# First attention of a two-layer kernel: probabilities scaled one period later, a shorter first guess, the bias as a matrix product

## The reference, cut to what matters

```python
q = _ln((x @ Wq + bq).reshape(b, s1, H, HD), qn_w, qn_b)
k = _ln(kv[..., :HD], kn_w, kn_b)        # the first 48 keys of a batch
k_dca = _ln(kv_dca[:, :, 0], kn_dca_w, kn_dca_b)   # its last 16 keys
...
ctx = _attn(qT, k, v)                    # softmax over 48 keys
ctx_dca = _attn(qT, k_dca, v_dca)        # softmax over 16 keys
return (ctx + ctx_dca) @ Wo + bo
```

## Time and profile before

| | |
|---|---|
| median of 3 runs | 749.72 us (747.78 to 749.95) |
| the profiled execution | 747.85 us, its span 746.0 us |
| busy in the span | PE 668.1, DVE 556.2, ACT 480.1, POOL 442.4 us |
| mean granted clock of TensorE | 0.979 of 2.4 GHz |

### The profile page before, as it was taken

How to read it: one execution, slowest core, us unless ns; L and a number is a source line. 1 busy time by engine, 2 the same in 40 slices (tenths; PEclk the granted TensorE clock), 3 DMA queues, 4 the chain that set the end, 5 groups by cost and what they waited for, 6 DMA issues and landing times. The chain is left out here.

```text
span 746.0 us, 16279 instructions
## 1 busy us (share of the span) xinstructions
PE 668.1 (90%) x5782; PEld 532.3 (71%) x5782; DVE 556.2 (75%) x1212; ACT 480.1 (64%) x982; POOL 442.4 (59%) x648
## 2 busy tenths in 40 slices
PE   2778888877999989999999999999999999978794
PEld 1556666655888877888888888888888888765452
DVE  3699999996578886768677777676777666746886
ACT  1467767664556667666666666666666666657994
POOL 2487787876677744656666666666656564535500
PEclk9999999996999999999999999999999999999996
DMA  8200000400410000000010000000000000000001
GB/s 285 61 9 9 9 8 12 169 1 2 127 58 29 8 15 1 16 22 16 15 29 9 22 23 22 23 16 15 29 9 15 15 2 1 1 1 1 29 29 58
DMA packets 26019, 22.83 MB, mean 31 GB/s; under 512 B 5041, under 2 KB 24402, under 8 KB 25810
## 3 DMA queue, kind: packets, MB, share of 16 engines
q1 hardware_dynamic: 24160, 20.92, 8.9%
q10 hardware_dynamic: 1778, 0.86, 0.4%
HBM read 19.67 MB, written 2.10 MB: 29 GB/s over the span
## 5 line engine op out<-in xcount | busy, mean ns | idle before, releaser
L683 POOL TENSOR_TENSOR rstd<-var,minus_half 128x8 f32<-128x8 f32 x65 | 107.7, 1657 | 5.1
L674 POOL TENSOR_TENSOR p_n<-pr,pinv 128x256 f32<-128x256 f32 x64 | 39.3, 613 | 79.6 <-DVE pinv L915 79.6
L659 POOL TENSOR_TENSOR pr<-pr,rstd 128x256 f32<-128x256 f32 x64 | 39.2, 613 | 78.7 <-DVE pr L954 78.7
L1565 PE MATMUL banks<-m_hi,z_hi 128*128 128x256 f32 x256 | 74.4, 291 | 7.5 <-DVE z_lo L907 7.5
L1193 ACT ACTIVATE kT<-banks,gk_q 128x512 f32<-128x512 f32 x64 | 44.0, 688 | 50.6 <-PE banks L1574 50.6
L1565 PE MATMUL banks<-m_hi,z_lo 128*128 128x256 f32 x256 | 72.1, 282 | 0.0
L1565 PE MATMUL banks<-m_lo,z_hi 128*128 128x256 f32 x256 | 72.0, 281 | 0.0
L907 DVE TENSOR_TENSOR z_lo<-banks,z_hi 128x512 fp32r<-128x512 f32 x64 | 43.9, 686 | 31.2 <-ACT z_hi L1159 31.2
L934 DVE TENSOR_REDUCE sums<-q_sq 128x4 f32<-128x512 f32 x64 | 43.7, 683 | 25.8 <-ACT q_sq L1174 25.7
L950 DVE TENSOR_REDUCE pmax<-banks 128x4 f32<-128x256 f32 x64 | 27.0, 422 | 46.3 <-PE banks L1610 46.3
L1565 PEld LDWEIGHTS banks<-m_hi,z_hi 128*128 128x128 f32 x256 | 48.3, 189 | 17.3 <-DVE z_lo L907 15.9
(11 more groups left out here) (189 smaller groups left out, 2087.8 us busy)
## 6 DMA issues: line engine op xcount, KB each, us to landing
w_raw<-in_L_xattn_Wq SPq DMA_DIRECT2D x4, 512.0 KB, 5.5
wo_raw<-in_L_xattn_Wo SPq DMA_DIRECT2D x1, 2048.0 KB, 8.3
k_ctx<-in_ctx SPq DMA_DIRECT2D x16, 128.0 KB, 2.7
w_raw<-in_L_ffn_w_gating SPq DMA_DIRECT2D x16, 128.0 KB, 2.4
out_x<-x_sb SPq DMA_DIRECT2D x4, 512.0 KB, 3.0
x_sb<-in_x SPq DMA_DIRECT2D x1, 1536.0 KB, 9.2
a_ctx<-in_ctx SPq DMA_DIRECT2D x16, 64.0 KB, 1.7
w_raw<-in_L_xattn_Wk SPq DMA_DIRECT2D x2, 512.0 KB, 8.9
```

Of the source, the lines that this page charges most:

```text
L674: pool.tensor_tensor(p_n[:, 1 - par, :, :], pr[:, 1 - par, :, :], pinv[:, 1 - par, :].unsqueeze(2).to_broadcast([P, HC, S]), ALU.mult).the ...
L683: pool.tensor_tensor(rstd1[:, par, :], var1[:, :], minus_half[:, :].to_broadcast([P, 2 * HC]), ALU.pow).then_inc(root1, 1)
L1565: last = nc.tensor.matmul(bank[6][:, za * D:(za + 1) * D], z[:, odd, c, :], mm[:, h, :], start=w % NS == 0 and c == 0 and m == 0, stop=w % ...
```

## The change

- `first_guess` has four steps instead of six, and with the reduction in front of it five. The factor 0.5 / 16 comes in through the scale of ScalarE's square, the constant through a 17th column of `qk_sq` that is set once; the reduction writes `half` itself, and the shift and the subtraction become one multiplication by -0.5 with an addition.
- GpSimd multiplies the probabilities of tile i - 1 (before: i) in step i, right behind the scaling of the heads and ahead of the rounding. It no longer adds the output bias to x.
- On TensorE, the turning of probabilities and all that follows it work on tile i - 2 (before: i - 1). The turning of the heads moves ahead of the product by the values, and the output product goes from before the values and scores to the end of the step. It begins with a product of a row of ones by the bias row, which waits for nothing from ScalarE.
- The product by the values goes to bank 4. Values have a third buffer, `v_blk2`. VectorE's update of x is at tile i - 3. ScalarE copies the first keys ahead of the square and the output at the end of its step. The loop has one step more.

Left out below are the names of the new semaphores and lines that do not change.

```diff
@@ -38,6 +38,7 @@
 SCALE0 = HD0 ** -0.5
+SQ_SCALE = (0.5 / HD0) ** 0.5
 PAD = 32
@@ -204,7 +205,9 @@
         rnd2 = sb(sa, "rnd2", [P, 2, W_CHUNK, 2])
-        r_room = sb(sa, "r_room", [P, 6 * D])
+        v_blk2 = sb(sa, "v_blk2", [P, PER, H // 2, 2 * HD0])
+        qk_sq = sb(sa, "qk_sq", [P, 2 * H, HD0 + 1])
+        r_room = sb(sa, "r_room", [P, 480])
         bo_bc = sb(sa, "bo_bc", [P, D])
@@ -220,12 +223,12 @@
         prm = sb(sa, "prm", [P, D])
-        b_room = sb(sa, "b_room", [P, 128])
+        ones_row = sb(sa, "ones_row", [P, P])
...
         qk_cent = sb(sa, "qk_cent", [P, 2, 2 * H, HD0])
-        qk_sq = sb(sa, "qk_sq", [P, 2 * H, HD0])
+        s_room = sb(sa, "s_room", [P, 2 * D])
         qk_norm = sb(sa, "qk_norm", [P, 2 * H, HD0])
@@ -380,12 +383,16 @@
-        A_FIRST, A_LAST = -3, NT + 2
-        LN_N, NEWT_N = 7, 8
+        A_FIRST, A_LAST = -3, NT + 3
+        LN_N, NEWT_N = 5, 8
...
-            return bank[2 if t < NT - 1 else 5]
+            return bank[2 if t < NT - 2 else 5]
+        def values(t):
+            return v_blk2 if t % 3 == 2 else v_blk[:, t % 3]
@@ -404,18 +411,14 @@
-        def first_guess(dve, base, half, total, y, tmp):
-            dve.tensor_scalar(half, total, 0.5 / HD0, 0.5 * QK_EPS, ALU.mult, ALU.add).then_inc(ln_steps, 1)
+        def first_guess(dve, base, half, y, tmp):
+            dve.tensor_scalar(y.bitcast(U32), half.bitcast(U32), -0.5, RSQRT_MAGIC_HALF, ALU.mult, ALU.add).then_inc(ln_steps, 1)
             dve.wait_ge(ln_steps, base + 1)
-            dve.tensor_scalar(y.bitcast(U32), half.bitcast(U32), 1, None, ALU.logical_shift_right).then_inc(ln_steps, 1)
+            dve.tensor_tensor(tmp, y, y, ALU.mult).then_inc(ln_steps, 1)
             dve.wait_ge(ln_steps, base + 2)
-            dve.tensor_scalar(y.bitcast(U32), y.bitcast(U32), -1.0, RSQRT_MAGIC_HALF, ALU.mult, ALU.add).then_inc(ln_steps, 1)
+            dve.scalar_tensor_tensor(tmp, tmp, -1.0, half, ALU.mult, ALU.mult).then_inc(ln_steps, 1)
             dve.wait_ge(ln_steps, base + 3)
-            dve.tensor_tensor(tmp, y, y, ALU.mult).then_inc(ln_steps, 1)
-            dve.wait_ge(ln_steps, base + 4)
-            dve.scalar_tensor_tensor(tmp, tmp, -1.0, half, ALU.mult, ALU.mult).then_inc(ln_steps, 1)
-            dve.wait_ge(ln_steps, base + 5)
             dve.scalar_tensor_tensor(y, tmp, 1.5, y, ALU.add, ALU.mult).then_inc(ln_steps, 1)
@@ -587,6 +590,9 @@
             pool.memset(v_blk[:], 0.0).then_inc(zeros, 1)
+            pool.memset(ones_row[0:1, :], 1.0).then_inc(ones_set, 1)
+            pool.memset(v_blk2[:], 0.0).then_inc(zeros, 1)
+            pool.memset(qk_sq[:, :, HD0:HD0 + 1], 0.5 * QK_EPS).then_inc(eps_set, 1)
             roots(pool, 0, 0)
@@ -604,6 +610,13 @@
                                        rstd2[:, t % 2, :, 0].unsqueeze(2).to_broadcast([P, 2 * H, HD0]), ALU.mult).then_inc(scaled, 1)
+                t = i - 1
+                if live(t, NT):
+                    pool.wait_ge(inv_ready, t + 1)
+                    for seg, (lo, hi) in enumerate(((0, MAIN), (MAIN, S))):
+                        pool.tensor_tensor(prob[:, t % 2, :, lo:hi], prob[:, t % 2, :, lo:hi],
+                                           sinv[:, t % 2, seg, :].unsqueeze(2).to_broadcast([P, H, hi - lo]), ALU.mult).then_inc(prob_ready, 1)
                 for c in chunks(i - 1):
@@ -611,20 +624,6 @@
                     pool.tensor_tensor(w0[:, part], w0_raw[:, part], rnd2[:, c % 2, :, 0], ALU.subtract).then_inc(w0_steps, 1)
-                t = i - 1
-                if live(t, NT):
-                    if t == 0:
-                        pool.wait_ge(bo_ready, 1)
-                    pool.wait_ge(xhat_ready, t + 1)
-                    pool.tensor_tensor(x_sb[:, t, :], x_sb[:, t, :], bo_bc[:, :], ALU.add).then_inc(x_biased, 1)
-                t = i
-                if live(t, NT):
-                    pool.wait_ge(inv_ready, t + 1)
-                    for seg, (lo, hi) in enumerate(((0, MAIN), (MAIN, S))):
-                        pool.tensor_tensor(prob[:, t % 2, :, lo:hi], prob[:, t % 2, :, lo:hi],
-                                           sinv[:, t % 2, seg, :].unsqueeze(2).to_broadcast([P, H, hi - lo]), ALU.mult).then_inc(prob_ready, 1)
                 if -1 <= i < NG - 2:
@@ -751,11 +750,13 @@
+                    if t == 0:
+                        dve.wait_ge(eps_set, 1)
                     dve.wait_ge(sq_ready, t + 1)
                     after(dve, scaled, t - 1)
-                    dve.tensor_reduce(qk_mean[:, :], qk_sq[:, :, :], AX.X, ALU.add).then_inc(ln_steps, 1)
+                    dve.tensor_reduce(half2[:, t % 2, :, 0], qk_sq[:, :, :], AX.X, ALU.add).then_inc(ln_steps, 1)
                     dve.wait_ge(ln_steps, LN_N * t + 1)
-                    first_guess(dve, LN_N * t + 1, half2[:, t % 2, :, 0], qk_mean[:, :], rstd2[:, t % 2, :, 0], qk_tmp[:, t % 2, :])
+                    first_guess(dve, LN_N * t + 1, half2[:, t % 2, :, 0], rstd2[:, t % 2, :, 0], qk_tmp[:, t % 2, :])
                 for c in chunks(i):
@@ -775,11 +776,10 @@
                                           smax[:, seg, :].unsqueeze(2).to_broadcast([P, H, hi - lo]), ALU.subtract).then_inc(shifted, 1)
-                t = i - 2
+                t = i - 3
                 if live(t, NT):
...
                     dve.wait_ge(y_done, t + 1)
-                    dve.wait_ge(x_biased, t + 1)
                     dve.tensor_tensor(x_sb[:, t, :], y_bank(t)[:, 0:D], x_sb[:, t, :], ALU.add).then_inc(x_updated, 1)
@@ -1031,7 +1031,7 @@
             normalised(0)
-            act.wait_ge(zeros, 3)
+            act.wait_ge(zeros, 4)
@@ -1059,14 +1059,14 @@
                     act.wait_ge(v_done, t + 1)
-                    after(act, o_done, t - 1)
+                    after(act, o_done, t - 2)
                     for odd in range(2):
                         keys = slice(odd * S, (odd + 1) * S)
-                        act.activation(v_blk[keys, t % 2, :, :, odd * HD0:(odd + 1) * HD0],
+                        act.activation(values(t)[keys, :, :, odd * HD0:(odd + 1) * HD0],
                                        bank[7][keys, 0:D].rearrange("p (b r d) -> p b r d", b=PER, d=HD0), ACT.Copy).then_inc(v_ready, 1)
...
                     normalised(i + 3)
-                t = i - 1
+                t = i - 2
                 if live(t, NT):
@@ -1079,11 +1079,6 @@
                     act.activation(prob[:, t % 2, :, :], prob[:, t % 2, :, :], ACT.Exp, scale=SCALE0).then_inc(exp_ready, 1)
-                t = i - 1
-                if live(t, NT):
-                    act.wait_ge(o_done, t + 1)
-                    after(act, y_done, t)
-                    act.activation(oT[:, :, :].rearrange("p k n -> p (k n)"), bank[7][:, D:2 * D], ACT.Copy).then_inc(o_evac, 1)
                 t = i + 1
@@ -1094,15 +1089,20 @@
                                    scale=cols[:, 0, 0:1], bias=cols[:, 0, 1:2]).then_inc(t_evac, 1)
+                    turned_keys(t, 0)
                 t = i + 2
...
                     after(act, ln_steps, LN_N * (t - 1) + 1)
-                    act.activation(qk_sq[:, :, :], qk_cent[:, t % 2, :, :], ACT.Square).then_inc(sq_ready, 1)
+                    act.activation(qk_sq[:, :, 0:HD0], qk_cent[:, t % 2, :, :], ACT.Square, scale=SQ_SCALE).then_inc(sq_ready, 1)
                 t = i + 1
                 if live(t, NT):
-                    turned_keys(t, 0)
                     turned_keys(t, 1)
+                t = i - 2
+                if live(t, NT):
+                    act.wait_ge(o_done, t + 1)
+                    after(act, y_done, t)
+                    act.activation(oT[:, :, :].rearrange("p k n -> p (k n)"), bank[4][:, 0:D], ACT.Copy).then_inc(o_evac, 1)
             run_steps(A_FIRST, A_LAST, step)
@@ -1302,11 +1302,11 @@
             def step(i, k):
-                t = i - 1
+                t = i - 2
                 if live(t, NT):
...
                     pe.wait_ge(prob_ready, 2 * (t + 1))
-                    pe.wait_ge(t_evac, 5 * min(t + 2, NT))
+                    pe.wait_ge(t_evac, 5 * min(t + 3, NT))
                     for hp in range(H // 2):
@@ -1327,23 +1327,40 @@
                         turned(n, bank[n], f_xhat, f_xhat_ready, fT_done, None)
+                if i == -1:
+                    pe.wait_ge(prm_in, PRM_DMAS * 16)
+                    for kk in range(KD):
+                        last = nc.tensor.transpose(bank[4][:, kk * PRM:(kk + 1) * PRM], prm[0:PRM, kk * P:(kk + 1) * P], ident[0:PRM, 0:PRM])
+                    last.then_inc(cols_done, 1)
                 if i == 0:
...
                     last.then_inc(bo_done, 1)
-                t = i - 1
+                t = i + 1
+                if live(t, NT):
+                    pe.wait_ge(scaled, t + 1)
+                    after(pe, pt_evac, 2 * (t - 2))
+                    for s in range(2):
+                        for c in range(KD):
```

(47 more changed lines are left out.)

## The result

The changed kernel takes 766.54 us (median of 6 runs, 761.80 to 767.29), the kernel before 749.87 us beside it. The ratio is 1.0208, with a 95% interval of 1.0187 to 1.0229: **slower by 2.1%**, where no measurable change was predicted. The profiled execution of the changed kernel is the fastest of the six (761.80 us); four of them took 765.9 to 767.3.

A forecast was written before the change was run, and what follows sets the result against it. VectorE was taken to bound the 9.32 us period. Gains at the start and in the loop were repaid at the end: feed-forward at 187.9 against 188.02 (-0.1), -0.3 with a clock chance, giving 749.4 us; range 745 to 753.

The forecast's parts named there:

- The stall behind L626: VectorE's L409 and L411 lie under GpSimd's products by the inverse sums; 1.2 us a period, to go with the change.
- GpSimd's chain: From the shift until TensorE can turn the heads: 9.7 us, needed at 10.5, so a margin of 0.8 us.
- VectorE's slack: VectorE's queue falls to 7.73 us in a period of 8.9, leaving 1.2 us to absorb any remaining stall.
- the bias: Product of ones by the bias row on TensorE, hidden by nothing: 0.46 us a period, bounds 0.28 and 0.53.
- turn to scores: Part of the loop through TensorE and ScalarE, from turning the heads to the scores: 3.23 us a period.
- the turning with both projections: Part of the same loop, turning of probabilities plus query and key products on TensorE: 2.75 us a period.
- The end: From tile 15's turn to the feed-forward's first product: near 27 us, paying back the six microseconds gained on the way.
- Tile 4's turn: Start of turning tile 4's heads, after the first tiles: 1.4 us earlier, at 62.8 instead of 64.24 us.
- eleven periods of 8.90: Loop from tile 4's turn to tile 15's, put at 160.7 us, 6.1 us before the 166.76 of the kernel before.
- rival 2: The end keeps the higher clock (-2.5 us) or the bias is nearly free (-2.0): 745 to 747 us; chance 0.22.
- Rival 4: The loop through the two probability buffers is longer than its sum, period 9.4: about 755 us; chance 0.20.
- the rule on transposes: Transposes do not count as busy for the clock, so last products at 1.2 GHz: feed-forward 1.0 us later, no measurable change.

The follow-up runs named there:

- with 128 rows: Changed kernel with the bias product over 128 rows of 1/128 instead of one row of ones: 743.49 us, ratio to the kernel before 0.9920.
- the long-guess kernel: Changed kernel with the bias product over 128 rows and the six-step first guess of the kernel before: 745.98 us, ratio to the kernel before 0.9938.
- the idle product: Changed kernel plus one 128-row, 256-column product of no use a period in TensorE's wait before the scores: 752.33 us, ratio to the kernel before 1.0023.
- the one-row control: Changed kernel plus a product of no use a period, over one row, in TensorE's wait before the scores: 760.61 us, ratio to the kernel before 1.0109.

## Why the prediction was wrong

**Right.** The stall behind L626 and its end; that the shift would wait for the turned probabilities (1.23 us for "about 1"); GpSimd's chain in time. VectorE's slack was tested and holds.

**Right in the sum, by luck in the terms.** The period at full clock is 8.93 for 8.90, because two terms were too low (the bias by 0.17, turn to scores by 0.11) and two too high (the output product by 0.10, the turning with both projections by 0.14). The end is 26.9 for 27.2 us with its clock the wrong way round: I had its first part at 1.2 GHz and its last two products at 2.4. The bias and output product of tile 14 took 1.59 us (190.62 to 192.21) and not 3.1, at full clock, and from the last product by the values to L1447 (195.19 to 198.86) were 3.67 us and not 1.85, at half clock and with a bias product for which that part of the sum had no term. Tile 4's turn is at 63.56 for 62.8; with 128 rows it is at 62.00, and most of the difference arises ahead of the first product with the bias.

**Wrong.** The step that failed is the product "eleven periods of 8.90". It took the full clock for all of them. The eleven took 108.4 and not 97.9 us: 10.5 more, of which 0.3 are 8.93 for 8.90 and the rest seven periods with a stretch at 1.2 GHz. I had asked of the clock only at the end, where TensorE has gaps, and even noted for rival 2 that the loop "leaves TensorE busier than now". It did, and the clock fell all the same. The sum goes on: L1447 is 11.0 us later than predicted (0.8 at tile 4, 10.5 in the loop, -0.3 at the end), and from there to the end of the span are 561.1 us instead of 558.0, of which 1.8 are the feed-forward's first 3.64 us at half clock. The rest, some 1.3, fits another stretch at half clock, from 673.6 to 677.0, which the kernel before does not have: the same copy of ScalarE (L1159) is 12.1 us behind that of the kernel before ahead of it (670.97 for 658.88) and 13.7 behind it after it (692.10 for 678.37). That makes the 14.0 us between the spans of 760.0 and 746.0. The difference of the medians is 2.7 more; four of the six runs have mean clocks of 0.946 to 0.948, against 0.954 in the profiled one.

**The cause.** My reading is that it depends on how much of the array is at work in the stretch from the value product to the bias product. In the new order there lie the turned rows, a value product over half the columns, a wait, scores over a quarter of the rows and then 0.63 us on a single row. Shown, for the loop from tile 4 to tile 15: with 128 rows there, or without the product, or with a full product in the wait, or with the output product moved into it, the falls are gone in the profiled execution; with one more product on a single row they stay; with 32 rows they are half as many; the same one-row product in the old order adds none to that of the kernel before. So the six long spacings take both, a product over few rows and the new order. A single fall comes without such a product too: the long-guess kernel, with its 128 rows, has one in the last period, where TensorE has fewer products. Each count is from one execution; the clocks of all executions bear it out with 128 rows (0.978 to 0.983, against 0.946 to 0.954 in the changed kernel) and less cleanly with the idle product (0.965 to 0.979). That the clock goes by the filled part of the array, and not by something else that rows change, is the simplest reading of these and not more.

The Trainium skill (TensorE: Matmul & The Clock Gate, Part 1) says that the clock follows "how busy the PE has been recently". Here TensorE was busy 2.9 of 3.6 us ahead of a fall, and in the one-row control 97.9% of the loop, with the clock at 0.89. If busy means time, the sentence does not fit these rows; if it means filled rows it does, and no run here shows what the chip counts.

**Rivals.** Rival 4 had the sign right and the place wrong: its loop is no longer than its sum. None of the rivals had a fall of the clock in the loop. By the rule on transposes the last products were to run at 1.2 GHz, and they did, against what I had read from the trace before. But the fall at 192.3 also follows 5.3 us in which TensorE was idle for 2.4, so these rows do not tell transposes from idle time.

**Without the fall** the prediction would still have been somewhat high: with 128 rows the kernel is 0.8% faster than before. The bias then costs 0.43 a period (8.74 against 8.31 without it).

## What to carry to other kernels

Ask of every product moved or added on TensorE not only how long it takes but what it fills, and what lies beside it: a bias by a product over one row can be spread over 128 rows at no cost, here 1.40 instead of 1.59 us with the output product, and 743.49 instead of 766.54 us in all. Look for the clock in the steady loop too, wherever small products, turnings and a wait come in a row, and spread the large products over the period. Here the stall between GpSimd and VectorE was not removed with the stalled instructions, since the next ones took it (0.4 of 1.6 us gained); it went when the long product was moved away.

## What was not expected of the hardware

- A one-row product of 256 columns is not cheaper than one over 128 rows, but dearer: 0.63 us from start to start against 0.54, and the output product behind it 0.96 against 0.86. With 32 rows it is 0.63 as well. Whether the rows themselves cost this or the change of shape between neighbours, no run tells.
- TensorE's clock fell to 1.2 GHz in a loop in which the engine hardly ever waits: with the idle one-row product it is busy 8.87 of 8.94 us in a period at full clock, and the clock falls in seven of the eleven periods.
- Extra work of no use made the changed kernel 14 us faster (752.33 against 766.54).
